# Two attention and expert layers on one core: the first router's check bounded by the spread of its weights

## What is computed

```
x = x + xattn0(layernorm(x), ctx)        # 16 heads
x = x + ffn0(layernorm(x))
x = x + xattn1(layernorm(x), ctx)        # one head
x = x + ffn1(layernorm(x))               # 8 experts, each takes its 256 best tokens

def ffn0(x):
    out_shared = square(relu(x @ Ws1)) @ Ws2
    logits = x @ Wr                              # 8 experts
    top_vals, top_idx = top_k(logits, 2)
    prob = trunc(onehot-weighted softmax(top_vals))
    return out_shared + sum over experts of prob * (square(relu(x @ W1)) @ W2)
```

## Time and profile before

| | |
|---|---|
| median of 3 runs | 242.64 us (242.48 to 245.16) |
| the profiled execution | 242.70 us |
| its span, first to last instruction | 240.8 us |
| PE busy | 199.2 us (83%), 1189 matmul records |
| DVE busy | 142.6 us (59%) |
| ACT busy | 93.7 us (39%) |
| POOL busy | 97.3 us (40%) |
| mean granted clock of TensorE | 0.987 |

### The profile page before, as it was taken

The page is one execution under the profiler, slowest core; times in us unless marked ns, Lnnn a source line. Parts: engine busy times, 40 slices in busy tenths (PEclk is TensorE's granted clock), DMA queues, the critical chain, the costliest instruction groups (busy, mean ns, idle before and its releaser), DMA issues.

```text
span 240.8 us, 3547 instructions
## 1 busy us (share of the span) xinstructions
PE 199.2 (83%) x1189; PEld 117.8 (49%) x1197; DVE 142.6 (59%) x530; ACT 93.7 (39%) x222; POOL 97.3 (40%) x107
## 2 busy tenths in 40 slices
PE   1697589998899969999899899988787987777760
PEld 0443235444454446726564367643235866666650
DVE  5899836832877297957655698788884621111110
ACT  2251135615262266315652433246763433322320
POOL 0428805200022502171209137650017768878743
PEclk9999999999999999999999999999999999999995
DMA  6510111100110000129920001210002322323222
GB/s 198 160 65 25 32 48 49 49 0 10 53 28 0 3 1 0 46 79 297 336 80 15 34 3 44 88 48 4 0 1 56 37 27 42 45 34 48 33 26 29
DMA packets 15193, 13.07 MB, mean 54 GB/s; under 512 B 3520, under 2 KB 12161, under 8 KB 15169
## 3 DMA queue, kind: packets, MB, share of 16 engines
q1 hardware_dynamic: 11440, 10.17, 13.5%
q0 software_dynamic: 3008, 2.31, 6.8%
q10 hardware_dynamic: 721, 0.30, 0.5%
HBM read 7.99 MB, written 3.21 MB: 47 GB/s over the span
## 4 chain that ended last, share of the span: by engine, by line
PE 36%; DVE 29%; POOL 10%; DMA 9%; issue 9%; ACT 5%; POOLq 1%; DVEq 0%; ACTq 0%
DMA out<-pT,idx 7%; PE psum L949 7%; POOL out L1848 5%; DVE rden L1456 4%; DVE mrow L1436 4%; PE psum L862 3%; PE psum L905 3%; DVE pT L1593 3%; PE psum L931 2%; DVE stats L1314 2%; PE psum L933 2%; PE psum L872 2%; PE psum L982 2%; DVE xn L1421 2%; PE psum L986 2%
## 5 line engine op out<-in xcount | busy, mean ns | idle before, releaser
L734 ACT ACTIVATE pT<-psum 103x512 f32<-103x512 f32 (+1 forms) x48 | 28.3, 598 | 39.1 <-PE psum L933 38.9
L1757 POOL TENSOR_SCALAR ve<-mv 128x4 f32<-128x4 f32 (+1 forms) x19 | 4.4, 229 | 95.5 <-DVE mv L1317 95.4
L862 PE MATMUL psum<-c 128*128 128x512 bf16 x115 | 29.4, 379 | 1.6 <-ACT key_map L758 1.0
L1436 DVE TENSOR_REDUCE mrow<-psum 128x4 bf16<-128x308 f32 x64 | 27.3, 468 | 5.4 <-PE psum L905 5.2
L1848 POOL DMA_INDIRECT out<-pT,idx x16 | 25.5, 1594 | 10.2 <-DVE pT L1660 6.8
L1840 POOL DMA_INDIRECT pT<-gather_rows,idx x16 | 17.7, 1106 | 23.7 <-DVE idx L1647 19.5
L1658 DVE TENSOR_TENSOR pT<-psum,b_rows 128x256 f32<-128x256 f32 (+1 forms) x9 | 3.5, 394 | 35.8 <-PE psum L1270 35.8
L905 PE MATMUL psum<-k_stack,q_stack 128*128 128x308 f16 x64 | 16.4, 298 | 6.3 <-DVE mrow L1436 5.8
L1258 PE MATMUL psum<-xinT,w 128*128 128x256 f32 (+1 forms) x72 | 16.2, 368 | 4.3 <-ACT xinT L818 3.6
L931 PE MATMUL psum<-q_stack,k_stack 128*103 128x512 f16 (+1 forms) x48 | 18.8, 393 | 0.5 <-DVE mT L1441 0.5
L1456 DVE RECIPROCAL rden<-psum 128x512 f32<-128x512 f32 (+1 forms) x5 | 13.6, 2713 | 9.6 <-PE psum L949 9.6
(11 more groups left out here) (197 smaller groups left out, 378.2 us busy)
## 6 DMA issues: line engine op xcount, KB each, us to landing
w<-in_L_ffn_W SPq DMA_DIRECT2D x16, 256.0 KB, 5.8
gather_rows<-xrow SPq DMA_DIRECT2D x4, 272.0 KB, 2.1
x<-in_x SPq DMA_DIRECT2D x4, 256.0 KB, 4.2
out<-res SPq DMA_DIRECT2D x4, 256.0 KB, 2.0
q_stack<-q_hi SPq DMA_DIRECT2D x24, 32.0 KB, 1.8
q_stack<-q_lo SPq DMA_DIRECT2D x24, 32.0 KB, 1.8
b_rows<-in_L_ffn_b SPq DMA_DIRECT2D x1, 512.0 KB, 3.6
pT<-gather_rows,idx POOLq DMA_INDIRECT x16, 2.6
```

Source lines behind the costliest of these rows:

```text
L734: nc.scalar.activation(pT[0:n, b % 2, s, :], ST_ps[s % 2][0:n, :], ACT.Exp).then_inc(exp_done, 1)
L862: pe.matmul(bank[b][:, :], ident16, c16[:, 0:4 * P], start=True, stop=True)
L1436: dve.tensor_reduce(mrow[:, b % 2, j, g * GH:(g + 1) * GH], S_ps[u % 2][:, 0:GK].rearrange("p (h k) -> p h k", h=GH), X, ALU.max).then_inc ...
```

## The change

The logits of the first router are no longer computed. The gap between two logits of a token is a sum over 128 features of the normalised feature times the difference of two router weights. The absolute values of a token's normalised features sum to at most 128, so if in every row of the router's weights the largest minus the smallest is under 15.9 / 128, no gap reaches 15.9. That is what is now put to the test, once, on the weights (128 rows of 8), instead of on the logits of all tokens.

So `route0`, `tops`, the tile `top0`, the semaphores `lg0_ps_done` and `top0_done` and PE's wait for the latter go, and so does the centring of the first router's weights; the check's own instructions are others. Nothing changes its place otherwise, and the general path is as before. Core of the diff:

```diff
+SPREAD_MAX = 15.9 / D
...
-                        nc.scalar.copy(w_c[:], tail2_ps[:, 0:F0 + 2 * E])
+                        nc.scalar.copy(w_c[:], tail2_ps[:, 0:F0 + E])
...
                         pe.wait_ge(res2_done, b)
-                        pe.wait_ge(top0_done, b)
...
-            def route0(u, j0, j1, ps):
-                for j in range(j0, j1):
-                    ins = pe.matmul(logits(ps[0])[:, j, :], xnT[:, 1, j * P:(j + 1) * P], w_c[:, F0:F0 + E], start=True, stop=True)
-                ins.then_inc(lg0_ps_done, 1)
...
-                        for n in range(2):
-                            pe.matmul(tail2_ps[:, F0 + n * E:F0 + (n + 1) * E], centre[:], w_r[:, n, :], start=True, stop=True)
+                        pe.matmul(tail2_ps[:, F0:F0 + E], centre[:], w_r[:, 1, :], start=True, stop=True)
...
                     if t >= 0 and s == 7:
                         hidden(t, 0, J, tail1_ps)
-                        route0(t, 0, J, tail1_ps)
...
             hidden(ua, a0, a1, aps)
-            route0(ua, a0, a1, aps)
             hidden(ub, b0, b1_, bps)
-            route0(ub, b0, b1_, bps)
             shared(ua, a0, a1, aps)
...
-            def tops(t, u, j0, j1, ps):
-                dve.wait_ge(lg0_ps_done, u + 1)
-                for j in range(j0, j1):
-                    ins = dve.max(top0[:, t * J + j, :], logits(ps[0])[:, j, :])
-                ins.then_inc(top0_done, 1)
...
-                        if t >= 0 and s == 8:
-                            tops(t, t, 0, J, tail1_ps)
...
-                tops(B - 1, ua, a0, a1, aps)
                 scale2(B - 1, ua, a0, a1, aps1)
                 scale2(B - 1, ub, b0, b1_, bps1)
-                tops(B - 1, ub, b0, b1_, bps)
                 share(B - 1, ua, a0, a1)
...
-                    settle(dve.tensor_tensor(scratch[:, 0:NT], top0[:, :, 0], top0[:, :, 1], ALU.subtract))
-                    settle(dve.tensor_tensor(scratch[:, NT:2 * NT], scratch[:, 0:NT], gain1[:], ALU.mult))
-                    settle(dve.tensor_tensor(scratch[:, 0:NT], scratch[:, 0:NT], scratch[:, NT:2 * NT], ALU.mult))
-                    settle(dve.tensor_scalar(scratch[:, 0:NT], scratch[:, 0:NT], 256.0, None, ALU.is_lt))
-                    any_false(scratch[:, 0:NT], 3)
+                    settle(dve.tensor_reduce(suspect[:, 5:6], w_r[:, 0, :], X, ALU.min))
+                    settle(dve.tensor_scalar(scratch[:, 0:E], w_r[:, 0, :], suspect[:, 5:6], SPREAD_MAX, ALU.subtract, ALU.is_lt))
+                    any_false(scratch[:, 0:E], 3)
```

More of the change, by code:

```diff
@@ L172, in program @@
         bq_rows = sb("bq_rows", [P, P])
-        w_c = sb("w_c", [P, F0 + 2 * E])
+        w_c = sb("w_c", [P, F0 + E])
         wq1_T = sb("wq1_T", [P, P])
@@ L182, in program @@
         hid2 = sb("hid2", [F0, T])
-        top0 = sb("top0", [P, NT, E])
         p1 = sb("p1", [P, J, NK])
@@ L274, in program @@
         wo_ps_done, res1_done, res0_done = sem("wo_ps_done"), sem("res1_done"), sem("res0_done")
-        lg0_ps_done, top0_done, hid_ps_done, hid_done, hid2_done = (sem(n) for n in ("lg0_ps_done", "top0_done", "hid_ps_done", "hid_done", "hid2_done"))
+        hid_ps_done, hid_done, hid2_done = (sem(n) for n in ("hid_ps_done", "hid_done", "hid2_done"))
         ffn_ps_done, res2_done = sem("ffn_ps_done"), sem("res2_done")
@@ L1015, in route1 @@
                 for j in range(j0, j1):
-                    ins = pe.matmul(logits(ps)[:, j, :], xnT[:, 3, j * P:(j + 1) * P], w_c[:, F0 + E:F0 + 2 * E], start=True, stop=True)
+                    ins = pe.matmul(logits(ps)[:, j, :], xnT[:, 3, j * P:(j + 1) * P], w_c[:, F0:F0 + E], start=True, stop=True)
                 ins.then_inc(lg1_ps_done, 1)
```

## The result

The changed kernel takes 241.74 us at the median of 20 runs (239.06 to 244.37), the kernel before 242.63 us (241.45 to 245.16, 20 runs beside them). The ratio is 0.995 with an interval of 0.993 to 0.9969: 0.8 to 1.7 us less. The shift is real and small. The forecast was 2.62 us less and a time of 240.0; the time came out 0.14 us above the top of the range.

A forecast was written before the change was run, and what follows sets the result against it. No single engine was taken as the bound: the chain is shared over several. Terms 0.96 + 0.33 + 0.21 + 0.33 + 0.16 + 0.13 + 0.50 = 2.62 us, from 242.64 to 240.0 us; range 238.6 to 241.6.

The forecast's parts named there:

- Once-only, 0.13: Centring of the first router's weights (half of line 1103) goes: 0.13 us less, 0.20 at most.
- Batch 0, 0.96: Router matmuls removed from PE at 69 to 76 us, nothing else late: 0.96 of 0.99 us comes free.
- Batches 1 and 2, 0.33 and 0.21: Router matmuls removed, but line 1010 waits for ScalarE's copy behind its square: 0.33 and 0.21 us gained of 0.99 each.
- Batch 3, 0.33 + 0.16: Last batch, in halves: 0.33 us from PE's work moving up, 0.16 from half b's top-eight in front of the last shares.
- The check, 0.50: VectorE, between second and third expert group: four instructions for six save 0.50 us, with 0.93 of room before the scatter.
- slower: PE's clock falls: Rival, chance 0.03: longer PE waits before line 1010 halve the clock; slower only if over 7.5 us of work ran so.
- the start of line 992 in batch 0: Sign: the shared expert's second product starts about 1.0 us earlier, with no new idle time in front of it.
- PE's waits for line 711 in batches 1 and 2: Sign: line 1010 shows PE idle, released by ScalarE's copy, and starts 0.3 and 0.2 us nearer to line 982.
- VectorE's order in half a: Sign: in the last batch, the shared sum of half a still follows VectorE's own work.
- the third group's sum: Sign: behind the check, this expert group's sum starts about 0.5 us nearer to the second's.
- a granted clock under 1.00 ahead of the last 10 us: Sign that would make the forecast wrong: PE's clock below full before the last 10 us.
- nearly all is absorbed: Rival, chance 0.15: VectorE could take batch 0's gain, leaving 1.3 us less, 241.3 us; 241.8 without the check's share.

The follow-up runs named there:

- after_again: The changed kernel run once more, nothing altered; the profiled execution took 241.93 us, ratio 0.9916 to the kernel before.
- gap_fill: The changed kernel plus useless matmuls in PE's waits near 87 us (seven) and near 29 us (five): 240.43 us against 244.00 for the kernel before.
- check_only: The kernel before with only the check's new lines, router matmuls and top-eight instructions kept: 242.50 us against 242.90.
- gap_fill_again: The changed kernel with PE's waits near 87 and 29 us filled with useless matmuls, run a second time: 239.59 us, ratio 0.9889 to the kernel before.
- gap87_only: The changed kernel with useless matmuls only in PE's wait near 87 us: 239.68 us, ratio 0.9878 to the kernel before.
- gap_fill_before: The kernel before with useless matmuls in PE's waits near 87 and 29 us: 243.63 us, ratio 0.9984 to the unfilled kernel before.

## Why the prediction was right or wrong

**The sum, term by term.** The mechanism was right: instructions on the chain that the trace prices at 0.99 us for eight give up that much where nothing else is late. Undisturbed, the change brings 2.9 us by the traces and 3.2 by the medians, where the sum said 2.62.

- *Once-only, 0.13.* Measured 0.23. The chain in time of `after_again` has 0.18 us on the product that was 0.40 in the earlier trace rows; I had taken off an overlap of the loads with their neighbours that isn't there.

```profile
53.23 0.18 PE psum L1096 x2
```

- *Batch 0, 0.96.* Measured 0.89. From the hidden product to the shared one (lines 982 and 992 before, 981 and 986 after) were 72.27 - 68.41 = 3.86 us, and are now 2.97; no new idle time stands in front of it, and VectorE's maxima still wait for PE and not the other way:

```profile
69.03 1.07 PE L981 MATMUL psum<-xnT,w_c 128*64 128x512 f32 x2
...
70.84 1.85 DVE L1420 TENSOR_REDUCE mrow<-psum 128x4 bf16<-128x308 f32 x4 [0.48 <-PE psum L905]
...
72.00 1.16 PE L986 MATMUL psum<-w_s,hid 64*128 64x128 f32 x8
```

  The idle time ahead of the maxima went from 1.38 to 0.48: 0.90 of it used, as the step said.
- *Batches 1 and 2, 0.33 and 0.21.* Without the fall 0.45 and 0.34, each 0.12 to 0.13 more: the new wait of PE for ScalarE's copy is there, as forecast, but shorter. In `gap_fill`, batch 1, then batch 2:

```profile
93.55 0.63 ACT L699 ACTIVATE hid<-hid 64x512 f32<-64x512 f32 x1
...
94.09 0.56 ACT L711 COPY p1T<-psum 77x512 f32<-77x512 f32 x1
...
94.70 1.16 PE L1004 MATMUL psum<-v,p1T 77*128 77x128 f32 x8 [0.37 <-ACT p1T L711]
```

```profile
118.53 0.63 ACT L699 ACTIVATE hid<-hid 64x512 f32<-64x512 f32 x1
119.06 0.56 ACT L711 COPY p1T<-psum 77x512 f32<-77x512 f32 x1
...
119.68 1.16 PE L1004 MATMUL psum<-v,p1T 77*128 77x128 f32 x8 [0.79 <-ACT p1T L711]
```

  The step put the copy 0.02 behind the end of the square (93.55 + 0.63 = 94.18). It starts at 94.09, 0.09 before that end, and in batch 2 0.10 before it: where nothing but the engine's own order holds it, ScalarE takes the next instruction 0.09 to 0.10 us ahead of the reported end of the last.
- *Batch 3, 0.33 + 0.16.* Measured 0.50. Counted from half a's reciprocal (135.87 before, 136.36 after), the shared product of half a starts 0.68 us earlier (7.76 instead of 8.44; the step said 0.66), that of half b is held by ScalarE's square and starts 0.4 to 0.5 earlier, and VectorE's sum starts at 9.11 instead of 9.19: it follows its own work, as told. The gain comes out at the next place where VectorE waits for PE:

```profile
144.12 1.42 PE L986 MATMUL psum<-w_s,hid 64*128 64x128 f32 x8 [0.38 <-ACT hid L699]
...
150.19 0.50 DVE L1342 SCALAR_TENSOR_TENSOR p<-psum,rstd,key_bias 128x77 f32<-128x77 f32 x2 [0.25 <-PE psum L992]
```

  From the reciprocal of half a to this line are 150.19 - 136.36 = 13.83 us, 14.24 before: 0.41 of the 0.50 is in by then. VectorE's wait is 0.25 there where the earlier trace rows has 0.33. The last 0.1 to 0.16 is the top-eight of half b, which is gone from the chain.
- *The check, 0.50.* 0.45 in the trace after and 0.14 in `check_only`. The failed part is the room in front of the scatter: 0.93 counted from the landing, of which about 0.8 is POOL's own way from a landing to its next start. The earlier trace rows is a line of the chain itself, so the landing was the last to come there, or level with VectorE: a sign that little room was left.

**The step that failed** is one of the rivals: "slower: PE's clock falls". It was weighed only as a case that decides for "slower", from 7.5 us of PE work at the lower clock, with a chance of 0.03, and dismissed by the earlier trace rows. Both were wrong turns. A fall needs no 7.5 us to matter: one stretch of 3.4 us costs 1.55 us, more than half the sum, and so belonged among the terms, not among the cases that end on the other side. And the earlier trace rows shows one execution, and the wrong stretch: it is granted 1.00 in `after_again` too, which falls right behind it. The page of before had no low slice ahead of its last, but its 242.48 to 245.16 in three runs held the hint that some executions pay over 2 us more. The Trainium skill ("TensorE: Matmul & The Clock Gate", HAM oscillation — how this bites in real kernels) warns of idle gaps between groups of matmuls, but of longer ones than this wait. The trace agrees that a gap can cost the clock, and differs in that 1.85 us were enough, in a wait that the change didn't lengthen, only moved.

The place was wrong as well: I looked for the fall in front of line 1010, where the change makes new waits (0.37 and 0.79 us), and it came behind the old wait of 1.85 us.

In the range, the low end as worded adds up to 2.62 + 0.67 + 0.6 less, 238.75 us, not 238.6; nothing hangs on it.

Of "what would show it", three of the signs came (the start of line 992 in batch 0, PE's waits for line 711 in batches 1 and 2, VectorE's order in half a), the third group's sum stood 0.46 nearer, and the last sentence, a granted clock under 1.00 ahead of the last 10 us, is the one that came true. The rival "nearly all is absorbed" gave the right number, 241.3 to 241.8, for a wrong reason: VectorE took nothing of batch 0's gain.

**The balance.** 239.6 (`gap_fill_again`) is what the kernel takes with the clock held up; 241.05 is what it took on the same chip without; and the kernel before took 242.45. So of 2.9 us, 1.5 are given back at the median: half of the gain to be had hung on the lines that fill a wait (three of them in `gap87_only`, 239.68).

## What to carry to other kernels

A change that takes work off PE moves every later wait of PE in time, and the granted clock can fall behind one that was harmless before. Price that as a term of the sum (here 1.55 us for one low stretch of 3.4 us, times how often it is to be expected), and read it from the spread of the runs as much as from the one profile. Where PE stands idle for 1 to 2 us between busy stretches, try matmuls that write nothing of use, released by a semaphore that comes early in the idle time. In the wait near 87 us they held nothing up and returned 1.4 us, as much as the change had brought on that chip; in the one near 29 us they brought nothing that the runs show.

## What was not expected of the hardware

- The clock fell to 1.2 GHz behind a wait of 1.85 us, in stretches of 3.3 to 3.4 us; one of these cost 1.55 us. The kernel before has about the same wait (1.86 us, 1.13 us later behind the start of phase 0), yet 25 of 107 executions below 0.987 against 35 of 41 of the changed kernel. Five useless matmuls 55 us ahead of it, which put it 1.06 us later, brought 10 of 12 to 0 of 6. The Trainium skill (same page, What's actually happening) says that the chip's look at the activity runs freely and so differs between runs of one kernel; that would fit the share. It would not by itself make a place within the kernel matter, and no run here shows it.
- ScalarE starts a copy 0.09 to 0.10 us before the reported end of the activation ahead of it.
- POOL starts a scatter 0.82 us after the landing of the scatter that it waits for (193.85 to 194.67 in `check_only`, 195.31 to 196.13 in `gap_fill_before`).
- Eight router products with eight new weights cost 0.99 us on the chain, and taking them out brought 0.89 us in the batch where nothing else was late.
